# Output projection of the self attention: one fp32 product, or three products of high and low parts in the rounded fp32 type

## The chip, the cores and the metric

The kernel runs on one core of one Trainium2 chip. The time is device time of one execution, in microseconds (us); the median of several runs is compared. Engines: TensorE (PE, with its weight loads as PEld), VectorE (DVE), ScalarE (ACT), GpSimd (POOL) and SyncE (SP), which issues most DMAs. Each engine works through its own queue in order, and the queues meet in semaphores.

## The reference, cut to what matters

x is [8, 512, 256] in fp32. A cross attention to a small context is added to x first. Then a layer of two paths is added, a dense one and a sparse one (a mixture of 8 experts, two of them for each token). The change lies in the dense path:

```python
q, k, v = x @ wq, x @ wk, x @ wv                    # 16 heads of 16
attn = softmax(mask(q k^T / 4))
o = (attn @ v).reshape(b, s, d)                     # [tokens, 256]
h = x + rmsnorm(o @ wo, attn_norm_w)                # o @ wo: the product that changes
ffn = silu(h @ w1) * (h @ w3) @ w2
return h + rmsnorm(ffn, ff_norm_w)
```

## The kernel before

All loops over batches are written out. `in_batches` makes one walk for each step of a software pipeline: a walk (b, c) does the first half of batch b (cross attention, q, k and v, routing, row maxima of the scores) interleaved with the second half of batch c = b - 1 (scores, softmax, output projection, dense network). The first walk has no c, and one more at the end has no b. Behind them come the experts' tiles (`tiles`), and an ending. One list, `STEPS`, gives the order in which every engine's queue takes the steps of a walk; each engine picks those steps in which it has work.

The steps around the change, in the order of the list:

- `cv`, the last product of the cross attention, and on DVE `norm_3`, which normalises the last of four token tiles (`normed`, L1408) once POOL has its reciprocal root (L663);
- `f_o_turn` (of c): PE transposes the attention's output `o_tok` into banks 6 and 7 (`turn`, L844, transposes with `ident`), and ACT copies it into `oT` (`spread`, L1146). `oT` is a part of `room`, a large tile that many stages share;
- `x2_turn` 0 and 1 (of b): the same for the normalised x, in two halves. The second half needs `norm_3`;
- `f_wo` 0 and 1 (L1031): the output projection. For each of four token tiles, 128x256 of output from two products over the halves of the inner dimension; stationary is `oT`, moving is `wo`, both fp32. It waits for both halves of `oT` (`oT_sb`, 2);
- `f_wo_sq`: squares and their sum on ACT (L1244), reciprocal root on POOL; `f_o_norm`: DVE multiplies (L1577) and POOL adds to the residual `hb` (L736); `f_h_turn`: `hb` is transposed and kept as a high part (ACT) and a low part (DVE, L1570) in the rounded fp32 type, called float32r in the code;
- `qk` 0 to 3 (L935): q and k of batch b. ACT, DVE and POOL split each into three bf16 parts, SP writes these to memory and DMAs bring them back spread over partitions (`rep_q`, `rep_k`);
- `v`, `route`, and `fu`/`fg`/`fd`, the dense network: its first product (L1051) is made of three terms, high by high, high by low and low by high, in float32r with 512 columns each;
- `max` (L969, L970): the scores' row maxima, from the parts that came back.

The order on PE is that of the list: what waits at `f_wo` 0 holds up `x2_turn` 1, `f_wo` 1, `qk` and all that follows. In the setup, SP loads the weights (L485: `wo`, `w2`), and in the first walk, ahead of `qk`, DVE reorders `wq` and `wk` (L1473) and scales three norm weights (L1476). POOL makes identity matrices and masks; `mask_kq` (L618, L623) is made and used by nothing.

Of the kernel before, what the change touches and what calls it, by code (L numbers as in the profile page):

```python
# [10 lines left out]
ALU = mybir.AluOpType  # L11
# [6 lines left out]
P = 128  # L18
# [41 lines left out]
    b_ps=G * UNITS, b_exp=G * UNITS, b_cut=G * UNITS, va_ps=G * CHUNKS, av_sb=4, avT_ps=4, o_rec=4, o_nrm=4,  # L60
    oT_ps=2, oT_sb=2, wo_ps=2, wo_sq=2, wo_ri=1, wo_n=2, hb=1, h=2, yb=1, hT_ps=2, hT_sb=2, hT_lo=2,
    fu_ps=16, fu_th=8, fu_u=8, fu_g=8, fd_ps=8, fd_sq=1, fd_ri=1, fd_n=1, y=1, y_out=16, pool_f=2,
# [144 lines left out]
def xattn_ffn(nc, A, out):  # L207
    per = PER
    counted = {}
    with ExitStack() as ctx:  # L210
        def sb(name, shape, dt=F32):
            return ctx.enter_context(nc.sbuf_tensor(name, shape, dt))

        def sem(name):
            return ctx.enter_context(nc.semaphore(name))
# [4 lines left out]
        kv_out = [sem(f"p0_kv_out{i}") for i in range(4)]  # L220
        p0 = {n: sem("p0_" + n) for n in ("w_first", "bias_ps", "w_early", "w_mid", "w_late", "w_turned", "w_up", "kv0_ps", "norms", "split_hi", "split", "ident", "const", "iota", "tr_ps", "tr_sb", "kv_ps", "kv_sb", "bk")}

# [10 lines left out]
        wv = sb("wv", [P, KD, D + E])  # L233
        wo = sb("wo", [P, KD, D])
        w1 = sb("w1", [P, 2, KD, FF], F32R)
# [11 lines left out]
        mask_qk = sb("mask_qk", [P, P], BF16)  # L247
        mask_kq = sb("mask_kq", [P, P], BF16)
        before_b = sb("before_b", [P, P], BF16)
# [17 lines left out]
        with nc.sbuf_tensor("hT", [P, 2, KD, S], F32R) as hT:  # L267
            pass
        room = sb("room", [P, 28672])

        def part(a, n):
            return room[:, a:a + n]
# [19 lines left out]
        scaled = part(3072, 1024).rearrange("p (t d) -> p t d", t=T)  # L292
        oT = part(4096, 1024).rearrange("p (k n) -> p k n", k=KD)
        xh = part(4096, 1024).rearrange("p (t d) -> p t d", t=T)
# [90 lines left out]
        def bank(i, n=512, at=0):  # L385
            return ps[:, i * 512 + at:i * 512 + at + n]
# [11 lines left out]
        def done(ins, name, n=1):  # L398

            counted[name] = counted.get(name, 0) + n  # L400
            return ins.then_inc(sems[name], n)

        def need(eng, b, name, k):

            eng.wait_ge(sems[name], b * per[name] + k + AHEAD.get(name, 0))
# [42 lines left out]
        def _(sp):  # L448
# [30 lines left out]
            def load_late_weights():  # L479
                for dst, src in ((w_heads[:, 0, :, :], "L0_ffn_wq"), (w_heads[:, 1, :, :], "L0_ffn_wk")):  # L480
                    sp.dma_start(dst, A[src].rearrange("(k p) n -> p k n", p=P)).then_inc(p0["w_late"], 16)
                sp.dma_start(wv[:, :, 0:D], A["L0_ffn_wv"].rearrange("(k p) n -> p k n", p=P)).then_inc(p0["w_late"], 16)
                sp.dma_start(wv[:, :, D:D + E], A["L0_ffn_router_w"].rearrange("(k p) n -> p k n", p=P)).then_inc(p0["w_late"], 16)
                for dst, src in ((wo, "L0_ffn_wo"), (w2, "L0_ffn_w2")):
                    sp.dma_start(dst[:, :, :], A[src].rearrange("(k p) n -> p k n", p=P)).then_inc(p0["w_late"], 16)  # L485
                for dst, src in ((aw_bc, "L0_ffn_attn_norm_w"), (fw_bc, "L0_ffn_ff_norm_w"), (mw_bc, "L0_ffn_moe_norm_w")):
                    sp.dma_start(dst[:, :], A[src].partition_broadcast(P)).then_inc(p0["w_late"], 16)
# [120 lines left out]
        def _(pool):  # L608
# [3 lines left out]
            for i, m in enumerate((ident, ident_b)):  # L612
# [3 lines left out]
                                pattern=[[-1, P]], channel_multiplier=1).then_inc(p0["ident"], 1)  # L616
            for m, x in ((mask_qk, 0.0), (mask_kq, 0.0), (before_b, 1.0)):
                g.memset(m[:, :], x).then_inc(p0["ident"], 1)  # L618
            pool.wait_ge(p0["ident"], 7)

            g.affine_select(out=mask_qk[:, :], in_=mask_qk[:, :], compare_op=ALU.is_ge, fill=MASKED, base=0,
                            pattern=[[-1, P]], channel_multiplier=1).then_inc(p0["ident"], 1)
            g.affine_select(out=mask_kq[:, :], in_=mask_kq[:, :], compare_op=ALU.is_ge, fill=MASKED, base=0,  # L623
                            pattern=[[1, P]], channel_multiplier=-1).then_inc(p0["ident"], 1)
            g.affine_select(out=before_b[:, :], in_=before_b[:, :], compare_op=ALU.is_gt, fill=0.0, base=0,
# [178 lines left out]
        def _(pe):  # L804
# [23 lines left out]
            pe.wait_ge(p0["w_mid"], 16 * 2)  # L828
            pe.wait_ge(p0["ident"], 10)
            pe.wait_ge(p0["const"], 9)  # L830
# [5 lines left out]
            def batch(b, c, end=False, only=None):  # L836
# [10 lines left out]
                for step in only or walked(b, c, end):  # L847
# [179 lines left out]
                    elif kind == "f_wo":  # L1027
                        need(pe, c, "oT_sb", 2)
                        for t in (2 * step[1], 2 * step[1] + 1):
                            for k in range(KD):  # L1030
                                last = mm(bank((6, 7)[t // 2], D, t % 2 * D), oT[:, k, t * P:(t + 1) * P], wo[:, k, :], start=(k == 0), stop=(k == KD - 1))  # L1031
                            if t % 2:
                                done(last, "wo_ps")
# [97 lines left out]
        def _(act):  # L1131
# [9 lines left out]
            def batch(b, c, end=False, only=None):  # L1141
                def spread(n, dst, banks, src_name, name, halves=(0, 1)):

                    for t2 in halves:
                        need(act, n, src_name, t2 + 1)
                        done(fn(dst[:, :, t2 * 2 * P:(t2 + 1) * 2 * P], bank(banks[t2]).rearrange("p (k n) -> p k n", k=KD), ACT.Copy), name)  # L1146

                for step in only or walked(b, c, end):
# [87 lines left out]
                    elif kind == "f_o_turn":  # L1236
                        if b is not None:
                            need(act, b, "sc_add", T)
                        spread(c, oT, (6, 7), "oT_ps", "oT_sb")
                    elif kind == "f_wo_sq":  # L1240
# [74 lines left out]
        def _(dve):  # L1315
# [72 lines left out]
            def batch(b, c, end=False, only=None):  # L1388
# [21 lines left out]
                for step in only or walked(b, c, end):  # L1410
# [56 lines left out]
                    elif kind == "qk":  # L1467
                        a = step[1]
                        if a == 0 and c is None:

                            dve.wait_ge(p0["w_late"], 16 * 9)
                            for i, w in enumerate((wq, wk)):
                                v.tensor_copy(w[:, :, :].rearrange("p k (a d h) -> p (k a) d h", a=KD, d=HD),  # L1473
                                              w_heads[:, i, :, :].rearrange("p k (a h d) -> p (k a) d h", a=KD, d=HD)).then_inc(p0["w_turned"], 1)
                            for w in (aw_bc, fw_bc, mw_bc):
                                v.tensor_scalar(w[:, :], w[:, :], float(D) ** 0.5, None, ALU.mult).then_inc(p0["norms"], 1)  # L1476
                            dve.wait_ge(p0["norms"], 3)
                        need(dve, b, "part1", a + 1)
# [79 lines left out]
                    elif kind == "out_t":  # L1558
# [5 lines left out]
                        done(v.tensor_tensor(o_tok[:, :, grp * 64:(grp + 1) * 64].rearrange("p t (j d) -> p t j d", j=4), t4[:, :, :, 0:HD],  # L1564
                                             orec[:, :, :].unsqueeze(3).to_broadcast([P, T, 4, HD]), ALU.mult), "o_nrm")
                    elif kind == "f_h_turn":
                        for t2 in range(2):
# [113 lines left out]
```

## Time and profile before

| | |
|---|---|
| median of 3 runs | 1482.12 us (1478.77 to 1482.25) |
| span of the profiled execution | 1484.5 us |
| PE busy | 1362.4 us, 92% |
| PE weight loads | 882.2 us, 59% |
| DVE, ACT, POOL busy | 810.0, 575.1, 600.2 us |
| mean granted TensorE clock | 0.976 |

The profiled execution is one of its own; its span is 1484.5 us, and the runs' times are of other executions of the same program. Busy time on PE is the union of the MATMUL records with modelled ends, so records that follow one another overlap: for the rate of a group, take the distances of starts. An fp32 product is recorded as two MATMULs with a weight load each, a float32r product or a transpose as one. The granted clock is 1.00 at 2.4 GHz and 0.50 at 1.2 GHz.

### The profile page before, as it was taken

Reading aid. Unit: us, or ns where it says so; the run is one execution under the profiler, and the core shown is the slowest. Engines: PE = TensorE matmul, PEld = TensorE weight load, DVE = VectorE, ACT = ScalarE, POOL = GpSimd, SP = SyncE. Lnnn points to the kernel's source line nnn. Section 1 sums busy time; section 2 is a strip of 40 time slices with the busy share of each in tenths; the row PEclk is TensorE's granted clock in tenths of the full one; section 3 lists DMA queues with packets and bytes.
Section 4 is the critical chain, followed back from the end, with each engine's and each line's share of the span. In section 5 each row is a group of like instructions: output and inputs, shape, how many; then the busy total and the mean of one; then the engine's idle time right before and its main releaser. Section 6 shows DMA issues by size and latency. Waiting matters only on the chain. (4 is left out here: it accounts for less than half of the span.)

```text
span 1484.5 us, 22385 instructions
## 1 busy us (share of the span) xinstructions
PE 1362.4 (92%) x7229; PEld 882.2 (59%) x7230; DVE 810.0 (55%) x1654; ACT 575.1 (39%) x1214; POOL 600.2 (40%) x1051
## 2 busy tenths in 40 slices
PE   6887899899999989998999899999999889999995
PEld 5543556666665666566656665666566346666674
DVE  2625554764585368536753675467537623333348
ACT  2231553055306521642265126503640443344446
POOL 4312353254325342634254225423542445555544
PEclk9998899999999999999999999999999899999997
DMA  6053204110501050106000500140022533322245
GB/s 213 1 153 132 86 1 121 52 30 1 142 30 30 1 156 16 30 8 160 20 15 30 141 17 15 51 121 17 1 83 74 162 107 128 129 87 85 85 186 193
DMA packets 78297, 115.39 MB, mean 78 GB/s; under 512 B 24840, under 2 KB 66208, under 8 KB 75648
## 3 DMA queue, kind: packets, MB, share of 16 engines
q1 hardware_dynamic: 67888, 79.69, 17.9%
q10 hardware_dynamic: 3840, 16.78, 4.2%
q0 software_dynamic: 6480, 17.77, 3.3%
q8 instruction: 52, 0.85, 0.2%
q14 instruction: 37, 0.30, 0.1%
HBM read 70.22 MB, written 43.59 MB: 77 GB/s over the span
## 5 line engine op out<-in xcount | busy, mean ns | idle before, releaser
L1540 DVE TENSOR_REDUCE nm<-ps 128x2 f32<-128x256 f32 (+3 forms) x256 | 202.5, 819 | 85.6 <-PE ps L970 79.5
L1229 ACT ACTIVATE room<-ps 128x512 f32<-128x512 f32 x320 | 179.8, 599 | 151.3 <-PE ps L996 151.1
L1051 PE MATMUL ps<-hT,w 128*128 128x512 f32 x768 | 206.5, 412 | 0.0
L703 POOL TENSOR_SCALAR_AFFINE_SELECT room<-room 128x256 f32<-128x256 f32 (+1 forms) x320 | 121.0, 390 | 136.4 <-ACT room L1229 131.7
L969 PE MATMUL ps<-room 96*128 96x128 bf16 (+3 forms) x512 | 127.9, 312 | 35.7 <-DMA room<-parts_d 17.8
L1051 PEld LDWEIGHTS ps<-hT,w 128*128 128x128 f32 x768 | 140.4, 190 | 32.1 <-DVE hT L1570 2.0
L1061 PE MATMUL ps<-w,room 128*128 128x256 f32 x512 | 137.8, 400 | 7.8 <-DVE room L1591 7.8
L1253 ACT ACTIVATE room<-ps 128x512 f32<-128x512 f32 x64 | 37.2, 593 | 277.2 <-PE ps L1051 277.2
L1087 PE MATMUL ps<-room 128*128 x284 | 135.4, 599 | 1.8 <-ACT room L1281 1.8
L920 PE MATMUL ps<-room 128*128 128x256 f32 x512 | 123.1, 384 | 2.8 <-ACT room L1190 1.8
L901 PE MATMUL ps<-room,xnT 128*128 128x512 f32 x256 | 122.0, 601 | 0.0
L996 PE MATMUL ps<-room 99*128 99x384 bf16 (+3 forms) x512 | 111.0, 306 | 8.7 <-ACT room L1229 6.4
L969 PEld LDWEIGHTS ps<-room 96*128 96x128 bf16 x512 | 50.9, 100 | 97.9 <-DVE nm L1540 41.1
L920 PEld LDWEIGHTS ps<-room 128*128 128x128 f32 x512 | 93.8, 190 | 22.7 <-issue 6.7
L1061 PEld LDWEIGHTS ps<-w,room 128*128 128x128 f32 x512 | 91.9, 195 | 24.1 <-DVE room L1591 11.5
L970 PE MATMUL ps<-mask_qk,ident_b 128*128 128x128 bf16 x512 | 104.6, 225 | 0.0
L1634 DVE COPY room<-ps 128x256 f32<-128x256 f32 x71 | 30.1, 424 | 125.9 <-PE ps L1095 117.7
L1441 DVE TENSOR_TENSOR room<-ps,room 128x1024 f32<-128x1024 f32 x32 | 39.1, 1222 | 106.0 <-PE ps L901 106.0
L996 PEld LDWEIGHTS ps<-room 99*128 99x128 bf16 x512 | 42.9, 98 | 88.0 <-issue 44.7
L1009 PE MATMUL ps<-room,v_aug 128*32 128x512 f32 (+3 forms) x1024 | 90.6, 449 | 3.0 <-POOL room L703 2.0
L652 POOL TENSOR_TENSOR spare_p<-neg_half 128x1 f32<-128x1 f32 x95 | 18.3, 192 | 179.7 <-DVE room L1533 114.6
L794 POOL DMA_INDIRECT pair_d<-room,ids_u x71 | 71.8, 1011 | 33.7 <-issue 30.5
(236 smaller groups left out, 2360.1 us busy)
## 6 DMA issues: line engine op xcount, KB each, us to landing
room<-parts_d SPq DMA_DIRECT2D x48, 256.0 KB, 8.7
room<-parts_d ACTq DMA_DIRECT2D x48, 256.0 KB, 6.2
room<-xs_d SPq DMA_DIRECT2D x71, 129.0 KB
parts_d<-room SPq DMA_DIRECT2D x64, 128.0 KB, 1.8
room<-pair_d SPq DMA_DIRECT2D x8, 1024.0 KB, 7.8
room<-in_L_ffn_ew SPq DMA_DIRECT2D x24, 256.0 KB, 5.5
xin<-in_x SPq DMA_DIRECT2D x8, 512.0 KB, 11.3
parts_d<-xnT SPq DMA_DIRECT2D x32, 128.0 KB, 1.8
```

Source lines behind the costliest of these rows:

```text
L703: done(g.affine_select(out=w, in_=w, compare_op=ALU.is_ge, fill=0.0, base=0, pattern=[[0, 2]] * (blocks - 1) + [[1, P]], channel_multiplie ...
L901: last = mm(bank(half), xnT[:, k, t * P:(t + 1) * P], m_sb[:, k, half * 512:(half + 1) * 512], start=(k == 0), stop=(k == KD - 1))
L920: last = mm(bank(3, D), pT[:, t % 2, a * P:(a + 1) * P], vw[:, a, :], start=(a == 0), stop=(a == PAIRS - 1))
L969: mm(bank(o, n), q_rep[0:KREP, rep_at(h), t * P:n], k_rep[0:KREP, rep_at(h), 0:n], start=True, stop=False)
L970: last = mm(bank(o, P, t * P), ident_b[:, :], mask_qk[:, :], start=False, stop=True)
L996: last = mm(ps[:, o:o + S - kb * P], k_rep[0:KREP + MROWS, h, kb * P:(kb + 1) * P], q_rep[0:KREP + MROWS, h, kb * P:S], start=True, stop=T ...
L1009: last = mm(ps[32 * j:32 * j + 32, 4 * 512 + kb * P:5 * 512], v_aug[:, v_at(kb, 4 * grp + j):v_at(kb, 4 * grp + j) + 32], prob[:, at:at + ...
L1051: last = mm(bank(up_banks(b, m)[i]), w[:, x, k, m * P:(m + 1) * P], hT[:, y, k, :], start=((x, y, k) == terms[0]), stop=((x, y, k) == term ...
L1061: last = mm(bank((6, 7)[half], D, t % 2 * D), gT[:, m % 2, t * P:(t + 1) * P], w2[:, m, :], start=(m == 0 and t % 2 == 0), stop=(m == FB - ...
L1087: last = mm(bank(2 + i % 2), xsT[:, i % 2, k * P:(k + 1) * P], ew[:, bass.ds(at + k * 2 * D, 2 * D)], start=(k == 0), stop=(k == KD - 1))
L1229: done(fn(prob[:, u * 512:(u + 1) * 512], bank(score_bank(b) + n % 2), ACT.Exp), "b_exp")
L1540: done(v.tensor_reduce(nm[:, t, 2 * hp:2 * hp + 2], pair_ps, AX.X, ALU.max, negate=True), "a_max")
```

## The change

`wo` is kept as a high part (the value rounded to float32r) and a low part (the rest). The fp32 matrix is loaded into a part of `room` (`wo_in`), and DVE makes the two parts in the first walk. `oT` becomes a high part, written by ACT in the same place as before, and a low part, which DVE makes in a new step of its own in `f_o_turn`: two subtractions of 128x512 from the banks. `f_wo` makes three terms for each half of the inner dimension: 6 products of 256 columns for a token tile where there were two fp32 ones, and waits for the low part (`oT_lo`, 2). The two new tiles lie in `room`'s space, which is laid over them. `mask_kq` goes, and one semaphore is used for two purposes.

```diff
--- before.py
+++ after.py
@@ -58,7 +58,7 @@
     gmax=1, gexp=1, mask=1, rank_ps=1, slot=1, xk=1, scat=128, dve_step=42, pool_a=4, pool_n=1,
     a_ps=32, a_max=32, m_part=2, mT_ps=2, mT_sb=2, m_row0=48, m_row1=48,
     b_ps=G * UNITS, b_exp=G * UNITS, b_cut=G * UNITS, va_ps=G * CHUNKS, av_sb=4, avT_ps=4, o_rec=4, o_nrm=4,
-    oT_ps=2, oT_sb=2, wo_ps=2, wo_sq=2, wo_ri=1, wo_n=2, hb=1, h=2, yb=1, hT_ps=2, hT_sb=2, hT_lo=2,
+    oT_ps=2, oT_sb=2, oT_lo=2, wo_ps=2, wo_sq=2, wo_ri=1, wo_n=2, hb=1, h=2, yb=1, hT_ps=2, hT_sb=2, hT_lo=2,
     fu_ps=16, fu_th=8, fu_u=8, fu_g=8, fd_ps=8, fd_sq=1, fd_ri=1, fd_n=1, y=1, y_out=16, pool_f=2,
 )
 
@@ -218,7 +218,7 @@
 
         sems = {n: sem(n) for n in per}
         kv_out = [sem(f"p0_kv_out{i}") for i in range(4)]
-        p0 = {n: sem("p0_" + n) for n in ("w_first", "bias_ps", "w_early", "w_mid", "w_late", "w_turned", "w_up", "kv0_ps", "norms", "split_hi", "split", "ident", "const", "iota", "tr_ps", "tr_sb", "kv_ps", "kv_sb", "bk")}
+        p0 = {n: sem("p0_" + n) for n in ("w_first", "bias_ps", "w_early", "w_mid", "w_late", "w_turned", "w_up", "kv0_ps", "split_hi", "split", "ident", "const", "iota", "tr_ps", "tr_sb", "kv_ps", "kv_sb", "bk")}
 
         moe = {n: sem("moe_" + n) for n in ("table_step", "table", "ids_off", "ids", "ew_in", "zero", "gate", "xT_ps", "xT", "up_ps", "th", "u", "g", "gT_ps", "gT", "dn_ps", "eo")}
         xs_in = [sem(f"xs_in{i}") for i in range(4)]
@@ -231,7 +231,7 @@
         wq = sb("wq", [P, KD, D])
         wk = sb("wk", [P, KD, D])
         wv = sb("wv", [P, KD, D + E])
-        wo = sb("wo", [P, KD, D])
+        wo = sb("wo", [P, 2, KD, D], F32R)
         w1 = sb("w1", [P, 2, KD, FF], F32R)
         w3 = sb("w3", [P, 2, KD, FF], F32R)
         w2 = sb("w2", [P, FB, D])
@@ -245,7 +245,6 @@
         ident = sb("ident", [P, P])
         ident_b = sb("ident_b", [P, P], BF16)
         mask_qk = sb("mask_qk", [P, P], BF16)
-        mask_kq = sb("mask_kq", [P, P], BF16)
         before_b = sb("before_b", [P, P], BF16)
         ones_b = sb("ones_b", [P, P], BF16)
         neg_half = sb("neg_half", [P, T])
@@ -266,6 +265,8 @@
 
         with nc.sbuf_tensor("hT", [P, 2, KD, S], F32R) as hT:
             pass
+        with nc.sbuf_tensor("oT_lo", [P, KD, S], F32R) as oT_lo, nc.sbuf_tensor("below_oT", [P, 3072], F32), nc.sbuf_tensor("oT_hi", [P, KD, S], F32R) as oT_hi:
+            oT = (oT_hi, oT_lo)
         room = sb("room", [P, 28672])
 
         def part(a, n):
@@ -290,7 +291,7 @@
         gT = part(3072, 1024).rearrange("p (i n) -> p i n", i=2)
         squares = part(2048, 1024).rearrange("p (t d) -> p t d", t=T)
         scaled = part(3072, 1024).rearrange("p (t d) -> p t d", t=T)
-        oT = part(4096, 1024).rearrange("p (k n) -> p k n", k=KD)
+        wo_in = part(22528, KD * D).rearrange("p (k n) -> p k n", k=KD)
         xh = part(4096, 1024).rearrange("p (t d) -> p t d", t=T)
 
         wq_c = part(11264, 2048).rearrange("p (k n) -> p k n", k=KD)
@@ -481,8 +482,8 @@
                     sp.dma_start(dst, A[src].rearrange("(k p) n -> p k n", p=P)).then_inc(p0["w_late"], 16)
                 sp.dma_start(wv[:, :, 0:D], A["L0_ffn_wv"].rearrange("(k p) n -> p k n", p=P)).then_inc(p0["w_late"], 16)
                 sp.dma_start(wv[:, :, D:D + E], A["L0_ffn_router_w"].rearrange("(k p) n -> p k n", p=P)).then_inc(p0["w_late"], 16)
-                for dst, src in ((wo, "L0_ffn_wo"), (w2, "L0_ffn_w2")):
-                    sp.dma_start(dst[:, :, :], A[src].rearrange("(k p) n -> p k n", p=P)).then_inc(p0["w_late"], 16)
+                for dst, src in ((wo_in, "L0_ffn_wo"), (w2[:, :, :], "L0_ffn_w2")):
+                    sp.dma_start(dst, A[src].rearrange("(k p) n -> p k n", p=P)).then_inc(p0["w_late"], 16)
                 for dst, src in ((aw_bc, "L0_ffn_attn_norm_w"), (fw_bc, "L0_ffn_ff_norm_w"), (mw_bc, "L0_ffn_moe_norm_w")):
                     sp.dma_start(dst[:, :], A[src].partition_broadcast(P)).then_inc(p0["w_late"], 16)
 
@@ -614,14 +615,12 @@
                 pool.wait_ge(p0["ident"], 2 * i + 1)
                 g.affine_select(out=m[:, :], in_=m[:, :], compare_op=ALU.not_equal, fill=1.0, base=0,
                                 pattern=[[-1, P]], channel_multiplier=1).then_inc(p0["ident"], 1)
-            for m, x in ((mask_qk, 0.0), (mask_kq, 0.0), (before_b, 1.0)):
+            for m, x in ((mask_qk, 0.0), (before_b, 1.0)):
                 g.memset(m[:, :], x).then_inc(p0["ident"], 1)
-            pool.wait_ge(p0["ident"], 7)
+            pool.wait_ge(p0["ident"], 6)
 
             g.affine_select(out=mask_qk[:, :], in_=mask_qk[:, :], compare_op=ALU.is_ge, fill=MASKED, base=0,
                             pattern=[[-1, P]], channel_multiplier=1).then_inc(p0["ident"], 1)
-            g.affine_select(out=mask_kq[:, :], in_=mask_kq[:, :], compare_op=ALU.is_ge, fill=MASKED, base=0,
-                            pattern=[[1, P]], channel_multiplier=-1).then_inc(p0["ident"], 1)
             g.affine_select(out=before_b[:, :], in_=before_b[:, :], compare_op=ALU.is_gt, fill=0.0, base=0,
                             pattern=[[1, P]], channel_multiplier=-1).then_inc(p0["ident"], 1)
             g.memset(neg_half[:, :], -0.5).then_inc(p0["const"], 1)
@@ -826,7 +825,7 @@
                         last = mm(bank(6 + i % 2, CK, a * CK), w[:, k, pa * P:(pa + 1) * P], ctxT[:, k, 0:CK], start=(k == 0), stop=(k == KD - 1))
                 last.then_inc(p0["kv0_ps"], 1)
             pe.wait_ge(p0["w_mid"], 16 * 2)
-            pe.wait_ge(p0["ident"], 10)
+            pe.wait_ge(p0["ident"], 8)
             pe.wait_ge(p0["const"], 9)
             pe.wait_ge(p0["iota"], 4)
 
@@ -1025,10 +1024,14 @@
                             before(pe, c, "fd_n")
                         turn(c, o_tok, (6, 7), lambda t2: [("o_nrm", G)], "oT_ps")
                     elif kind == "f_wo":
-                        need(pe, c, "oT_sb", 2)
+                        need(pe, c, "oT_lo", 2)
+                        if c == 0:
+                            pe.wait_ge(p0["w_turned"], 4)
+                        terms = [(x, y, k) for x, y in ((0, 0), (0, 1), (1, 0)) for k in range(KD)]
                         for t in (2 * step[1], 2 * step[1] + 1):
-                            for k in range(KD):
-                                last = mm(bank((6, 7)[t // 2], D, t % 2 * D), oT[:, k, t * P:(t + 1) * P], wo[:, k, :], start=(k == 0), stop=(k == KD - 1))
+                            for x, y, k in terms:
+                                last = mm(bank((6, 7)[t // 2], D, t % 2 * D), oT[x][:, k, t * P:(t + 1) * P], wo[:, y, k, :],
+                                          start=((x, y, k) == terms[0]), stop=((x, y, k) == terms[-1]))
                             if t % 2:
                                 done(last, "wo_ps")
                     elif kind == "f_h_turn":
@@ -1236,7 +1239,7 @@
                     elif kind == "f_o_turn":
                         if b is not None:
                             need(act, b, "sc_add", T)
-                        spread(c, oT, (6, 7), "oT_ps", "oT_sb")
+                        spread(c, oT[0], (6, 7), "oT_ps", "oT_sb")
                     elif kind == "f_wo_sq":
                         for i in range(2):
                             need(act, c, "wo_ps", i + 1)
@@ -1472,9 +1475,12 @@
                             for i, w in enumerate((wq, wk)):
                                 v.tensor_copy(w[:, :, :].rearrange("p k (a d h) -> p (k a) d h", a=KD, d=HD),
                                               w_heads[:, i, :, :].rearrange("p k (a h d) -> p (k a) d h", a=KD, d=HD)).then_inc(p0["w_turned"], 1)
+                            v.tensor_copy(wo[:, 0, :, :], wo_in).then_inc(p0["w_turned"], 1)
+                            dve.wait_ge(p0["w_turned"], 3)
+                            v.tensor_tensor(wo[:, 1, :, :], wo_in, wo[:, 0, :, :].bitcast(F32), ALU.subtract).then_inc(p0["w_turned"], 1)
                             for w in (aw_bc, fw_bc, mw_bc):
-                                v.tensor_scalar(w[:, :], w[:, :], float(D) ** 0.5, None, ALU.mult).then_inc(p0["norms"], 1)
-                            dve.wait_ge(p0["norms"], 3)
+                                v.tensor_scalar(w[:, :], w[:, :], float(D) ** 0.5, None, ALU.mult).then_inc(p0["w_turned"], 1)
+                            dve.wait_ge(p0["w_turned"], 7)
                         need(dve, b, "part1", a + 1)
                         if a >= 2:
                             need(dve, b, "part3", a - 1)
@@ -1563,6 +1569,12 @@
                         need(dve, c, "o_rec", grp + 1)
                         done(v.tensor_tensor(o_tok[:, :, grp * 64:(grp + 1) * 64].rearrange("p t (j d) -> p t j d", j=4), t4[:, :, :, 0:HD],
                                              orec[:, :, :].unsqueeze(3).to_broadcast([P, T, 4, HD]), ALU.mult), "o_nrm")
+                    elif kind == "f_o_turn":
+                        for t2 in range(2):
+                            need(dve, c, "oT_sb", t2 + 1)
+                            cols = slice(t2 * 2 * P, (t2 + 1) * 2 * P)
+                            done(v.tensor_tensor(oT[1][:, :, cols], bank(6 + t2).rearrange("p (k n) -> p k n", k=KD),
+                                                 oT[0][:, :, cols].bitcast(F32), ALU.subtract), "oT_lo")
                     elif kind == "f_h_turn":
                         for t2 in range(2):
                             need(dve, c, "hT_sb", t2 + 1)
```

## Rows read from the trace of the kernel before

**Rows 1.** Page, part 1: busy us, share of the span, instructions.

```profile
PE 1362.4 (92%) x7229; PEld 882.2 (59%) x7230; DVE 810.0 (55%) x1654; ACT 575.1 (39%) x1214; POOL 600.2 (40%) x1051
```

**Rows 2.** Windows, one walk: stretch, length, busy by engine, clock, DMA share.

```profile
597.00:740.00 143.00, 134.83 (x780) 89.35 (x780) 84.29 (x170) 55.27 (x111) 56.19 (x82) 1.00 0.19 53
```

**Rows 3.** Waits of PE: us in total, times, longest.

```profile
PE ps L969 <- DMA room<-parts_d: 17.8, 7, 3.8
```

**Rows 4.** Timeline around f_wo of one walk: start us, us, instructions, idle before.

```profile
227.35 1.04 PE L844 MATMUL ps<-ident,o_tok 128*128 128x128 f32 x8
228.04 1.08 ACT L1146 ACTIVATE room<-ps 128x512 f32<-128x512 f32 x2 [3.96 <-PE ps L844]
228.22 0.60 PE L844 MATMUL ps<-ident,xn_id 128*128 128x128 f32 x4
...
229.18 1.99 PE L1031 MATMUL ps<-wo,room 128*128 128x256 f32 x8 [0.36 <-ACT room L1146]
229.66 0.41 DVE L1408 TENSOR_SCALAR xn_id<-x,mv,rs 128x256 f32<-128x256 f32 x1 [0.71 <-POOL rs L663]
...
231.45 1.89 PE L1031 MATMUL ps<-wo,room 128*128 128x256 f32 x8
...
233.18 3.60 PE L935 MATMUL ps<-xn2T,wq 128*128 128x512 f32 x8
```

**Rows 5.** Source view of L1031: duration ns min/median/max, first and last start.

```profile
L1031 PE MATMUL ps<-wo,room x128: 379/379/484, 229.2 to 1205.0; 128*128 128x256 f32 x128
```

**Rows 6.** L1051 (float32r): timeline of PE, then its source view.

```profile
245.70 5.64 PE L1051 MATMUL ps<-hT,w 128*128 128x512 f32 x23
...
L1051 PE MATMUL ps<-hT,w x768: 388/397/776, 245.7 to 1461.0; 128*128 128x512 f32 x192
```

**Rows 7.** Timeline of L826, fp32 records of 64 columns.

```profile
14.82 7.36 PE L826 MATMUL ps<-room 128*128 128x64 f32 x64 [0.69 <-ACT room L1140]
```

**Rows 8.** Source view of L1570, the low part of hT.

```profile
L1570 DVE TENSOR_TENSOR hT<-ps,hT x16: 678/686/691, 244.4 to 1213.7; 128x512 fp32r<-128x512 f32 x16
```

**Rows 9.** Timeline, the low part of hT and the product behind it.

```profile
244.35 1.29 DVE L1570 TENSOR_TENSOR hT<-ps,hT 128x512 fp32r<-128x512 f32 x2 [2.16 <-ACT hT L1146]
...
245.70 0.50 PE L1051 MATMUL ps<-hT,w 128*128 128x512 f32 x1
```

**Rows 10.** Timeline, the projection's norm and the residual add.

```profile
234.64 1.02 POOL L663 TENSOR_TENSOR ri<-ve_f,neg_half 128x4 f32<-128x4 f32 x1
...
238.05 1.65 DVE L1577 SCALAR_TENSOR_TENSOR o_tok<-ps,ri,aw_bc 128x256 f32<-128x256 f32 x4
...
240.84 2.50 POOL L736 TENSOR_TENSOR hb<-hb,o_tok 128x512 f32<-128x512 f32 x2
```

**Rows 11.** Windows at three waits before max and behind them.

```profile
260.17:263.17 3.00, 0.00 (x1) 0.02 (x1) 0.51 (x3) 0.60 (x1) 0.19 (x1) 1.00 0.91 227
263.17:267.00 3.83, 3.82 (x16) 2.75 (x17) 1.42 (x3) 0.00 (x0) 1.08 (x1) 0.59 0.13 43
...
834.97:841.00 6.03, 6.03 (x22) 4.27 (x23) 2.30 (x4) 0.00 (x0) 2.04 (x2) 0.53 0.07 24
...
977.20:979.60 2.40, 0.06 (x2) 0.08 (x2) 0.50 (x3) 0.60 (x1) 0.19 (x1) 1.00 0.86 212
979.60:984.20 4.60, 4.60 (x19) 3.23 (x20) 2.30 (x4) 0.00 (x0) 1.70 (x2) 0.63 0.09 31
```

**Rows 12.** Windows at such a wait in another walk.

```profile
543.00:549.00 6.00, 2.77 (x17) 2.05 (x15) 2.62 (x15) 0.60 (x1) 0.19 (x1) 1.00 0.76 178
```

**Rows 13.** Timeline of the first walk: DVE at qk.

```profile
84.16 0.69 DVE L1481 SCALAR_TENSOR_TENSOR xin<-ps,xnT 128x512 f32<-128x512 f32 x1 [3.98 <-ACT xnT L1196]
```

**Rows 14.** Source view of L623, a mask.

```profile
L623 POOL TENSOR_SCALAR_AFFINE_SELECT mask_kq<-mask_kq x1: 292/292/292, 3.2 to 3.2; 128x128 bf16<-128x128 bf16 x1
```

**Rows 15.** Timeline of the last walk, around f_wo.

```profile
1200.52 1.09 ACT L1146 ACTIVATE room<-ps 128x512 f32<-128x512 f32 x2 [2.27 <-PE ps L844]
...
1206.27 0.41 PE L1078 MATMUL ps<-ident,room 128*128 128x128 f32 x2 [0.89 <-DMA room<-xs_d]
```

## The prediction

> **What bounds the kernel now.** I read four views, in this order. The page first: PE is busy 92% of the span, DVE 55%, and no other engine comes near [rows 1]. Then the table by walk: a walk of one batch takes some 143 us and PE is busy in about 135 of them; seven walks have this stretch and are alike, so one read closely stands for all [rows 2]. Then the releasers of PE's idle time: the largest is the first score product of the "max" stage (L969), 17.8 us in 7 times, on a DMA that brings q and k back [rows 3]. Last the timeline around the projection (L1031) in one walk [rows 4], where the argument is; the reader is to see that PE runs there with one idle stretch of 0.36 us, and which two rows of ACT and DVE stand beside it. The kernel is bound by PE in program order: what makes PE wait, or work longer, lengthens the walk unless a later wait swallows it.
>
> **What goes and comes on PE.** One fp32 product of 256 columns is two MATMUL records, so f_wo has 8 + 8 records in a walk. Eight of them take 1.89 us, of which 0.38 is the last one's own duration: (1.89 - 0.38) / 7 = 0.216 us apart, 16 x 0.216 = 3.46 us in a walk [rows 4, 5]. In the new form each token tile has 3 terms x 2 halves of the inner dimension = 6 records, 24 in a walk. The trace has no rounded product of 256 columns. The nearest rows: the rounded product of 512 columns, 23 records in 5.64 us, (5.64 - 0.40) / 22 = 0.238 apart [rows 6]; and the fp32 records of 64 columns with a weight load of 128 each, 64 in 7.36 us, (7.36 - 0.28) / 63 = 0.112 apart (twice 64 columns stream in 0.053, so that is the pace of the loads) [rows 7]. So a rounded record streams a column per cycle at 2.4 GHz (512 columns are 213 ns) with some 18 to 25 ns over it, where the fp32 one makes two passes of its 256. For 256 columns the stream is 107 ns, and I take 0.125 us apart (half of 0.213, and 0.018 over it, the nearest of the terms). The bounds are 0.112 (the pace of the loads) and 0.238 (the width doesn't matter). 24 x 0.125 = 3.00 us: PE saves 0.46 us in a walk, between 0.77 saved and 2.25 lost by the bounds.
>
> The Trainium skill ("TensorE: Matmul & The Clock Gate", Measured speedup vs the span model) says that a weight load overlaps matmuls in flight only when it targets other row groups; here all use all rows. By its load time (LDWEIGHTS section: 128 columns at 1.2 GHz, an estimate of 107 ns), load and stream would add to 0.214 us a record. The 0.238 us at 512 columns speaks against it: added, that would be 0.320.
>
> **The new wait.** Before, f_wo 0 began when ACT had copied both halves of the transposed output: copies 228.04 to 229.12, product at 229.18 [rows 4]. Now the low part has to be there too: two subtractions of 128x512 on DVE, the same operation as the low part of hT, mean 686 ns [rows 8]; the pair runs 1.29 us, and PE begins 0.06 us behind it (244.35 + 1.29 = 245.64, L1051 at 245.70) [rows 9]. They stand in DVE's queue behind norm_3, the last normalised token tile, which waits for POOL's reciprocal root and runs 229.66 to 230.07 [rows 4]. ACT's copies are done long before. So the subtractions run from 230.03 (DVE overlaps neighbours by some 0.05) to 231.32, and f_wo 0 begins at 231.38, not 229.18: **2.2 us later**. Queued behind it on PE: x2_turn 1, f_wo 1, qk. x2_turn 1 needs norm_3 (230.07) and could have run at once; it stands behind the waiting product and hides nothing. Until 231.38 PE has nothing else in its order.
>
> From f_wo 0 to qk it is 233.18 - 229.18 = 4.00 us now: 3.46 of products, and 0.54 of four transposes and the joints. It becomes 3.00 + 0.54 = 3.54. So qk begins at 231.38 + 3.54 = 234.92 instead of 233.18: **+1.74 us in a walk**.
>
> **Does a later wait give it back?** The only large one is the DMA before "max" (17.8 / 7 = 2.5 us in the mean, 3.8 at most) [rows 3]. It would, if that DMA were anchored ahead of f_wo. It isn't: what it brings are the parts of q and k, made from the products of qk by ACT, DVE and POOL and then written to memory, and the last two stand in POOL's queue behind the residual add (240.84), which needs the normed output of this same projection [rows 10]. qk, the parts, the DMA and max all move by the same 1.74 us. The norm of the projection (POOL's root, ready at 234.64 + 1.02 = 235.66) is used by DVE at 238.05, 2.4 us of slack; both ends move alike. Nothing late before is early now. Seven walks have this stretch (b = 1 to 7): 7 x 1.74 = **12.2 us**.
>
> **The clock.** The new gap of PE runs from the end of x2_turn 0 (228.82) to 231.38, 2.56 us, where it was 0.36. PE's granted clock is 1.00 in the walks but for a few drops to half (1.2 GHz), and those follow such gaps. Before "max": 3.00 us idle, then a mean of 0.59 over the next 3.83 us; some 2.3 us idle, then 0.63 over 4.6; and 0.53 over the 6.03 us behind the longest wait [rows 11]. A wait of some 3.2 us in another walk was followed by none [rows 12], and so were the remaining ones of the seven. Three drops from seven waits, all from waits above 2 us. Mine lies among the short ones, but transposes, not products, fill the 1.47 us before it. A drop costs half of what it covers, (1 - 0.63) x 4.6 = 1.7 us, and it would fall on dense products. I take 2 of 7: **3.4 us**; none to five is 0 to 8.5.
>
> **The edits outside.** The split of wo in the first walk is a copy and a subtraction of 128x512 on DVE (0.6 to 0.7 us each, by rows 8), some 1.3 us together, behind the copies that PE waits for and ahead of rest1, for which DVE idles 3.98 us until ACT's copy at 84.1 [rows 13]: nothing; uncovered it would be 1.3 once. The load of wo goes to another address with the same bytes; the mask's two POOL instructions go, the longer 0.29 us at 3.2 us of the span [rows 14], and PE doesn't wait for POOL in the setup: between 0 and 0.5 gained, I take 0. In the last walk, with no cross attention beside it, DVE is free: ACT's second copy ends at 1201.61 and the second subtraction at about 1202.45, so f_wo starts some 0.85 us later and saves 0.46; the 0.4 us left fall into the 0.89 us for which PE then waits for a DMA [rows 15]. Nothing.
>
> **Sum.** 12.2 + 3.4 = 15.6 us on the profiled span of 1484.5, which gives 1500.1. That execution is 2.4 us above the median of the runs, 1482.12; on the median it is 1497.7. I forecast **1498 us**.
>
> **Rivals.** (1) The rounded product at 256 columns costs as much as load and stream together, or its width doesn't matter: 0.216 to 0.238 a record. For: nothing in the trace shows this width. Against: the wider rounded products [rows 6] overlap their loads, and loads alone come every 0.112 [rows 7]. Then f_wo takes 5.2 to 5.7 us instead of 3.46, a walk grows by 2.2 + 1.7 to 2.2 = 3.9 to 4.4, seven by 27 to 31: 1509 to 1513, with the drops up to 1516. (The skill's rule on loads, were it true, is at the low end of this.) Chance 0.08.
> (2) The other side: the wait before "max" swallows the stall. If what ends last there is not the chain from qk but a DMA that stands on something earlier (the memory's pace, the SP queue), then PE reaches it 1.74 us later and waits up to 1.74 less. It decides from where the DMA's landing doesn't move with qk. For: the DMA share is 0.91 and 0.86 in two of these waits [rows 11], so the DMA engines are nearly full. Against: they are filled by this batch's own parts. The shorter gaps then also spare the three drops there, 5 us: 1477 to 1483. Chance 0.08, of which 0.04 faster and 0.04 the same.
> (3) My forecast's mechanism, with everything between no drop and five and 0.112 to 0.15 us a record: 7 x (2.2 - 0.77) = 10.0 without a drop, 1492.1; 7 x (2.2 + 0.15) = 16.5 with five drops, 1507. Chance 0.82. A remaining 0.02 is spread over surprises of both signs.
>
> **Range and chances.** 1489 to 1508 holds case 3 and a little; the two rivals outside are 0.16. About 0.3% (4.4 us) can be told from no change: faster 0.05, same 0.05, slower 0.90.
>
> **What would show it.** In the profile after: f_wo with 24 records in a walk, about 0.125 us apart, a PE gap of about 2.5 us before it put down to DVE's subtraction, DVE's pair of subtractions directly behind norm_3, qk 1.7 us later behind x2_turn 0, the wait before "max" unchanged at some 2.5 us, walks longer by 1.7 to 3.5 us, and half-clock stretches right behind f_wo's gap in one to four walks. The forecast is wrong if PE's gap before f_wo is under 1 us, if the records are 0.2 us apart, or if the wait before "max" shrinks by as much as qk moves.

## The result, and the profile after

| | before | after |
|---|---|---|
| median | 1482.18 us (4 runs) | 1502.23 us (4 runs, 1499.6 to 1509.8) |
| ratio of the times | | 1.0137 (95% interval 1.0102 to 1.0171) |
| span of the profiled execution | 1484.5 us | 1502.8 us |
| PE busy | 1362.4 us | 1372.2 us |
| mean granted clock | 0.976 | 0.966 |

The change makes the kernel 20 us slower. The forecast was 1498 us, slower with a chance of 0.90. One run of e3 below (1547 us) and one of the kernel before beside it (6109 us) were slow ones, and are left out of the medians and ratios.

Part 1 of the page after [rows 1 before]: PE is busy 10 us longer, with 64 records more, and DVE has 18 more, 16 of them the new subtractions and two the split of `wo`.

```profile
PE 1372.2 (91%) x7293; PEld 895.2 (60%) x7294; DVE 821.1 (55%) x1672; ACT 574.9 (38%) x1214; POOL 599.8 (40%) x1049
```

The waits of PE after (in total, times, longest) [rows 3 before]. A wait that was not there is now the largest: all eight f_wo wait for the low part, 19.1 us. The wait before max on the parts from memory is 13.8 us in 6 times, where it was 17.8 in 7.

```profile
PE ps L1033 <- DVE oT_lo L1576: 19.1, 8, 2.5
...
PE ps L968 <- DMA room<-parts_d: 13.8, 6, 2.9
```

The timeline around f_wo in one walk after (start us, us, count, idle before) [rows 4 before]. The reader is to see the order on DVE: norm_3 (L1411) behind its wait for POOL, then the two subtractions at once, then PE 0.05 us behind their end; and on PE nothing between the transposes of 520.78 and 523.88. ACT's copies had ended at 521.69.

```profile
519.91 1.04 PE L843 MATMUL ps<-ident,o_tok 128*128 128x128 f32 x8
...
520.61 1.08 ACT L1149 ACTIVATE oT_hi<-ps 128x512 fp32r<-128x512 f32 x2 [3.96 <-PE ps L843]
...
520.78 0.60 PE L843 MATMUL ps<-ident,xn_id 128*128 128x128 f32 x4
...
522.22 0.41 DVE L1411 TENSOR_SCALAR xn_id<-x,mv,rs 128x256 f32<-128x256 f32 x1 [0.71 <-POOL rs L662]
522.55 1.28 DVE L1576 TENSOR_TENSOR oT_lo<-ps,oT_hi 128x512 fp32r<-128x512 f32 x2
...
523.88 0.74 PE L1033 MATMUL ps<-wo,oT_hi 128*128 128x256 f32 x4 [2.50 <-DVE oT_lo L1576]
524.46 0.40 PE L1033 MATMUL ps<-wo,oT_lo 128*128 128x256 f32 x2
...
527.03 0.40 PE L1033 MATMUL ps<-wo,oT_lo 128*128 128x256 f32 x2
527.27 3.17 PE L934 MATMUL ps<-xn2T,wq 128*128 128x512 f32 x7
```

From f_wo 0 to the first product of qk it is 527.27 - 523.88 = 3.39 us here, where it was 4.00. But this is the one walk of seven where the clock held. Windows over the gap and over f_wo to qk, in the walk before and in this one (stretch, length, busy by engine, granted clock, DMA share): the same 28 records (24 products and 4 transposes) take 4.93 us at a mean clock of 0.65, or 3.39 at 1.00. The gap itself is 2.50 us in both.

```profile
372.92:375.42 2.50, 0.00 (x1) 0.00 (x0) 1.74 (x4) 0.80 (x2) 0.73 (x2) 1.00 0.02 7
375.43:380.36 4.93, 4.93 (x28) 4.93 (x29) 0.00 (x0) 1.22 (x5) 0.00 (x0) 0.65 0.00 0
521.38:523.88 2.50, 0.00 (x1) 0.00 (x0) 1.74 (x4) 0.80 (x2) 0.73 (x2) 1.00 0.00 0
523.88:527.27 3.39, 3.38 (x29) 3.39 (x29) 0.00 (x0) 1.22 (x5) 0.00 (x0) 1.00 0.00 0
```

The starts of the steps on PE, read from both traces for all seven walks with this stretch, split the walk in five. In us, before and after:

| stretch on PE | before, each walk | after, each walk | seven walks, after minus before |
|---|---|---|---|
| f_o_turn to f_wo 0 | 1.83 | 3.98 | +15.0 |
| f_wo 0 to qk | 4.00 | 3.38 once, 4.81 to 4.94 six times | +4.8 |
| qk to the dense network (first L1054) | 12.52 | 12.52 | 0.0 |
| dense network to max | 16.1 to 18.3 | 16.0 to 17.7 | -2.3 |
| max to the next f_o_turn | 77.4 to 109.4 | 77.3 to 109.6 | +1.0 |
| before the first and behind the last | | | -0.2 |

They sum to 18.3 us, the difference of the spans. The second line is two things: 7 x 0.62 = 4.3 us saved by the products, and 9.1 lost in six walks at half clock. The last three are small and of both signs; the stretches that differ between walks contain the wait for memory and an occasional drop of the clock. The -0.2 is -2.4 ahead of the first walk and +2.2 behind the last; the first f_o_turn starts anywhere from 222.6 to 227.3 us in the ten profiles of this case.

### The profile page after: what moved, and what is told of

Read it like the earlier page. It is cut to its first block and busy times, and to the rows that moved or that the text cites. A ratio compares the mean times of both kernels' runs of the same rounds, so it can differ in the third digit from the quotient of the medians.

```text
span 1502.8 us, 22530 instructions
## 1 busy us (share of the span) xinstructions
PE 1372.2 (91%) x7293; PEld 895.2 (60%) x7294; DVE 821.1 (55%) x1672; ACT 574.9 (38%) x1214; POOL 599.8 (40%) x1049
## 3 DMA queue, kind: packets, MB, share of 16 engines
q1 hardware_dynamic: 67888, 79.69, 17.7%
## 5 line engine op out<-in xcount | busy, mean ns | idle before, releaser
L1054 PE MATMUL ps<-hT,w 128*128 128x512 f32 x768 | 208.5, 415 | 0.0
L1054 PEld LDWEIGHTS ps<-hT,w 128*128 128x128 f32 x768 | 142.0, 192 | 32.6 <-DVE hT L1582 2.0
L651 POOL TENSOR_TENSOR spare_p<-neg_half 128x1 f32<-128x1 f32 x95 | 18.3, 192 | 182.2 <-DVE room L1539 117.1
```

What stands on the lines that cost most here:

```text
L1054: last = mm(bank(up_banks(b, m)[i]), w[:, x, k, m * P:(m + 1) * P], hT[:, y, k, :], start=((x, y, k) == terms[0]), stop=((x, y, k) == term ...
```

## The experiments

Theory A: the loss is PE's wait for DVE's low part, which ends 2.15 us behind the old start in each walk because the subtractions stand behind norm_3, and the half clock that follows the gap; the rounded products themselves save 0.62 us a walk. Theory B: the products are the costly part. Ratios are to runs of the kernel before on the same chip. The gap is PE's idle time just before f_wo 0; a drop is a stretch at half clock (1.2 GHz) that begins around the start of f_wo, behind that gap. Gaps, drops and the stretch f_wo to qk are read from each kernel's own trace, which is one execution; how many drops the other executions had is not known.

| kernel | median us | ratio (95%) | gap before f_wo | drops of 7 |
|---|---|---|---|---|
| changed, again | 1504.01 | 1.0129 (1.0080 to 1.0178) | 2.50 | 7 |
| e1 wait, fp32 products | 1503.95 | 1.0143 (1.0112 to 1.0175) | 2.50 | 3 |
| e2 no low part | 1478.07 | 0.9960 (0.9939 to 0.9981) | 0.36 | 0 |
| e3 gap filled | 1494.38 | 1.0085 (1.0052 to 1.0119) | filled, 0.61 left | 0 |
| e7 high terms first | 1479.70 | 0.9966 (0.9943 to 0.9988) | 0.36 | 0 |
| e4 low part ahead of norm_3 | 1486.30 | 1.0030 (1.0005 to 1.0054) | 1.38 | 0 |
| e5 half by half | 1499.32 | 1.0115 (1.0078 to 1.0152) | 1.90 | 6 |
| e6 both | 1479.95 | 0.9984 (0.9957 to 1.0010) | 0.78 | 0 |

The median of the kernel before was 1483.6 beside the first four (e1, e2, e3, e7) and 1483.1 beside the others.

**e1, the wait alone.** To the kernel before, the DVE step is added and f_wo waits for it:

```diff
-                        need(pe, c, "oT_sb", 2)
+                        need(pe, c, "oT_lo", 2)
...
+                    elif kind == "f_o_turn":
+                        for t2 in range(2):
+                            need(dve, c, "oT_sb", t2 + 1)
+                            cols = slice(t2 * 2 * P, (t2 + 1) * 2 * P)
+                            done(v.tensor_tensor(oT_lo[:, :, cols], bank(6 + t2)..., oT[:, :, cols], ALU.subtract), "oT_lo")
```

> The kernel before with only the low part and its wait: DVE makes the two subtractions of 128x512 in f_o_turn, f_wo waits for them and then makes the old fp32 products (the low part is used by nothing). Theory A (the wait for DVE, and the half clock behind it, make the loss; the rounded products save 0.62 us in a walk): the gap before f_wo is 2.5 us as in the changed kernel, f_wo to qk is 4.00 us where the clock holds and about 5.5 where it drops, so 7 x 2.15 = 15 us and 1.5 us for each drop; with six drops 1482 + 15 + 9 = 1506 us, between 1500 and 1510, some 4 us above the changed kernel. Theory B (the three rounded products are the costly part, the wait is mostly hidden): within 5 us of 1482.

1503.95 us. All of the loss is there without one rounded product. PE's wait is that of the changed kernel (L1571 is the new subtraction, whose tile lies in `room` here):

```profile
PE ps L1032 <- DVE room L1571: 19.1, 8, 2.5
```

Windows over f_wo to qk, in a walk at full clock and in one that drops to half:

```profile
517.54:521.54 4.00, 4.00 (x21) 3.54 (x22) 0.00 (x0) 1.33 (x5) 0.00 (x0) 1.00 0.00 0
662.24:667.91 5.67, 5.67 (x20) 4.77 (x21) 0.00 (x0) 1.32 (x5) 0.00 (x0) 0.70 0.00 0
```

Theory B is out. The 4 us that theory A expected above the changed kernel don't show in the times: the profiled execution had three drops where the changed kernel's had six and seven, and three or four drops less, at 1.5 us, are worth about as much as the 4.3 us that the rounded products save. But that execution was the second fastest of six (1501.41 us, granted clock 0.975); three others took 1505 to 1508 us at 0.969 or 0.970, so three drops need not be the usual number. Whether the same gap drops the clock less often ahead of fp32 products stays open.

**e2, the products alone.** DVE's step is left out, and the high part stands in for the low one:

```diff
-                        need(pe, c, "oT_lo", 2)
+                        need(pe, c, "oT_sb", 2)
...
-                                last = mm(..., oT[x][:, k, t * P:(t + 1) * P], wo[:, y, k, :],
+                                last = mm(..., oT[0][:, k, t * P:(t + 1) * P], wo[:, y, k, :],
```

> The changed kernel without the low part of oT: DVE's two subtractions are left out, f_wo waits for ACT's copies only, and the two products of low by high take the high part in the low part's place, so one term of the projection is wrong and all 24 records stay. Theory A: no gap, no drop behind it, f_wo to qk 3.4 us against 4.00: 1482 - 7 x 0.62 = 1478 us (1475 to 1480). Theory B: 24 records cost more than 16, above 1490 us.

1478.07 us, 5.5 below its kernel before (5.9 by the ratio); 7 x 0.62 = 4.3 were expected, inside the interval. No walk has a drop at f_wo, and f_wo to qk is 3.38 us in all seven:

```profile
511.94:515.32 3.38, 3.38 (x28) 3.38 (x29) 0.41 (x1) 1.66 (x6) 0.45 (x1) 1.00 0.00 0
653.84:657.22 3.38, 3.38 (x29) 3.38 (x29) 0.41 (x1) 1.66 (x6) 0.45 (x1) 1.00 0.00 0
```

**e3, the clock alone.** The wait stays; PE gets work in the gap:

```diff
+                        if step[1] == 0 and b is not None:
+                            for _ in range(34):
+                                mm(bank(4, P), ident_b[:, :], mask_qk[:, :], start=True, stop=True)
                         need(pe, c, "oT_lo", 2)
```

> The changed kernel, with 34 bf16 products of 128 columns (mask by identity, into a bank that nothing reads) put ahead of f_wo 0 in the seven walks, where PE waits anyway: some 1.9 us of work in a gap of 2.5. Nothing that f_wo waits for moves. Theory A with the clock as a cost of its own: no half clock at f_wo, f_wo to qk 3.4 us in all walks instead of 4.8 to 4.9 in six of seven: 6 x 1.45 = 8.7 us less, about 1493 us (1490 to 1496). Rival C (the drops cost nothing, since what follows waits for others): the time of the changed kernel, 1500 to 1504.

1494.38 us, inside the expected stretch. By the ratios it is 7.7 and 6.5 us below the two measurements of the changed kernel; 8.7 were expected. The interval of its ratio (to 1.0119) meets that of the first measurement (from 1.0102) and overlaps that of the second (from 1.0080), so the size is rough; the trace is not. The timeline of PE shows the filling, and f_wo at the same distance from the transposes as in the changed kernel:

```profile
514.34 2.06 PE L1029 MATMUL ps<-mask_qk,ident_b 128*128 128x128 bf16 x34
517.01 0.74 PE L1036 MATMUL ps<-wo,oT_hi 128*128 128x256 f32 x4 [0.61 <-DVE oT_lo L1579]
...
520.39 1.02 PE L934 MATMUL ps<-xn2T,wq 128*128 128x512 f32 x2
```

f_o_turn to f_wo 0 is 3.98 us as in the changed kernel, f_wo to qk 3.38 in all seven. What is left above the kernel before, 12.6 us by the ratio, is the wait less the saving: 15.0 - 4.3 = 10.7. So the clock is a loss of its own, and work that is used by nothing took it away.

**e4, DVE's order.** In walks with a second half, norm_3 moves behind the subtractions:

```diff
                     elif kind == "norm_3":
-                        normed(T - 1)
+                        if c is None:
+                            normed(T - 1)
...
                     elif kind == "f_o_turn":
...
+                        if b is not None:
+                            normed(T - 1)
```

> The changed kernel with DVE's order turned: in walks with a second half, norm_3 stands behind the two subtractions instead of ahead of them. Theory A (the stall is DVE's two subtractions plus the wait of norm_3 for POOL ahead of them): the subtractions run from 228.95 to 230.2 in the old walk's times, f_wo begins 1.1 us later than before instead of 2.15, the gap is 1.4 us, too short to drop the clock; a walk is 1.1 - 0.62 = 0.45 us longer than before, seven 3.2: 1483 + 3 = 1486 us (1484 to 1491). Theory A' (the subtractions alone are the stall, norm_3's place is nothing): as the changed kernel, 1500 to 1504.

1486.30 us, as expected. The timeline shows the subtractions in DVE's place of waiting for POOL, norm_3 behind them, and PE 1.1 us sooner:

```profile
516.16 1.28 DVE L1577 TENSOR_TENSOR oT_lo<-ps,oT_hi 128x512 fp32r<-128x512 f32 x2
...
517.35 0.40 DVE L1411 TENSOR_SCALAR xn_id<-x,mv,rs 128x256 f32<-128x256 f32 x1
...
517.49 0.74 PE L1033 MATMUL ps<-wo,oT_hi 128*128 128x256 f32 x4 [1.38 <-DVE oT_lo L1577]
```

Of the 16 to 18 us gained over the changed kernel 7.8 are the shorter wait (f_o_turn to f_wo 2.86 instead of 3.98, seven times); the rest, 8 to 10 us, is near what six or seven drops cost at 1.5 us, and none of the seven walks drops here.

**e5, half by half.** One word of the wait:

```diff
-                        need(pe, c, "oT_lo", 2)
+                        need(pe, c, "oT_lo", step[1] + 1)
```

> The changed kernel, with f_wo 0 waiting for the first half of the low part only and f_wo 1 for the second. Theory A: f_wo begins 0.63 us sooner than in the changed kernel, with a gap of 1.9 us; 1.5 - 0.62 = 0.9 us a walk above before, 6.4 in seven, 1489, and 1.5 for each drop of the clock that a gap of 1.9 us still brings (none to four): 1489 to 1495. Rival C (the gap's length does not matter to the clock): six drops, 1498.

1499.32 us. Theory A's range was missed: the wait is shorter by 0.6 us as expected, but a gap of 1.90 us still brought the half clock in six of seven walks. Rival C's number came out (six drops, 1498), its reason did not: in e4 and e6, where the gap is shorter still, none of the seven walks drops. The timeline of PE at such a gap,

```profile
518.48 0.75 PE L1033 MATMUL ps<-wo,oT_hi 128*128 128x256 f32 x4 [1.90 <-DVE oT_lo L1576]
```

and the windows over f_wo to qk in this walk and the next:

```profile
518.48:523.38 4.90, 4.90 (x28) 4.90 (x29) 0.54 (x1) 1.33 (x5) 0.00 (x0) 0.66 0.00 0
665.36:670.29 4.93, 4.93 (x28) 4.93 (x29) 0.54 (x1) 1.33 (x5) 0.00 (x0) 0.65 0.00 0
```

**e6, both of these.**

> Both: the subtractions ahead of norm_3, and each half of f_wo waits for its half. Theory A: the first subtraction ends at about 229.6, f_wo begins 0.45 us later than before and saves 0.62 behind it: 0.15 us a walk less, no drop: 1482 us (1479 to 1485), no difference from before that can be told. Rival D (x2_turn 1 or qk waits for the later norm_3): 0.5 us a walk more, 1486.

1479.95 us, as expected, and the same as before within the interval. The gap is 0.78 us, f_o_turn to f_wo 2.25, f_wo to qk 3.38 in the seven walks:

```profile
511.45 0.74 PE L1033 MATMUL ps<-wo,oT_hi 128*128 128x256 f32 x4 [0.78 <-DVE oT_lo L1577]
```

**e7, high terms first.** f_wo 0 makes the two terms of the high part for all four token tiles, f_wo 1 the term of the low part, into banks 4 and 5, so that DVE can still read banks 6 and 7:

```diff
-                        need(pe, c, "oT_lo", 2)
+                        low = step[1]
+                        need(pe, c, ("oT_sb", "oT_lo")[low], 2)
...
-                        terms = [(x, y, k) for x, y in ((0, 0), (0, 1), (1, 0)) for k in range(KD)]
-                        for t in (2 * step[1], 2 * step[1] + 1):
+                        terms = [(x, y, k) for x, y in (((0, 0), (0, 1)), ((1, 0),))[low] for k in range(KD)]
+                        for t in range(T):
                             for x, y, k in terms:
-                                last = mm(bank((6, 7)[t // 2], D, t % 2 * D), oT[x]...
+                                last = mm(bank((4, 5)[t // 2], D, t % 2 * D), oT[x]...
...
```

> The changed kernel with f_wo in another order and other banks: f_wo 0 makes the high-by-high and high-by-low terms of all four token tiles, into banks 4 and 5, and waits for ACT's copies only; then x2_turn 1; f_wo 1 makes the low-by-high terms, waiting for DVE. Theory A: 16 records (1.9 us) and four transposes (0.44) fill PE from 229.2 to 231.5, when the low part is just there; qk comes 0.6 us earlier than in the kernel before, no gap, no drop: 1482 - 4.3 = 1478 us (1475 to 1481). Rival D (the shared banks 4 and 5, or the wait of x2_turn 1 for norm_3, put a new wait in its place): 1482 or more.

1479.70 us, ratio 0.9966 (0.9943 to 0.9988): faster than the kernel before and than the changed one. The timeline: PE starts behind ACT's copies again, and by the time 16 records and four transposes are done the subtractions have ended (514.89), so the low terms wait for nothing that matters.

```profile
512.80 2.16 PE L1034 MATMUL ps<-wo,oT_hi 128*128 128x256 f32 x16 [0.36 <-ACT oT_hi L1150]
...
513.61 1.28 DVE L1577 TENSOR_TENSOR oT_lo<-ps,oT_hi 128x512 fp32r<-128x512 f32 x2
...
514.79 0.60 PE L843 MATMUL ps<-ident,xn_id 128*128 128x128 f32 x4
...
515.15 1.20 PE L1034 MATMUL ps<-wo,oT_lo 128*128 128x256 f32 x8
```

**The changed kernel again.**

> The changed kernel once more, for a second profile. Theory A: the gap of 2.50 us in all seven walks and f_wo to qk 3.38 where the clock holds, 4.8 to 4.9 where it drops; how many of the seven drop is left open, between three and seven. The span goes with that number, 1.5 us each.

1504.01 us; the profiled execution has the gap of 2.50 us and a drop in all seven walks, and a span of 1509.2, where the first had six and 1502.8. It was the slowest of its four runs; the fastest took 1497.03 us at a granted clock of 0.976, against 0.964 here, a sign that the number of drops varies from one execution to the next. Two of its windows, f_wo to qk:

```profile
377.84:382.76 4.92, 4.92 (x28) 4.92 (x29) 0.00 (x0) 1.33 (x5) 0.00 (x0) 0.65 0.00 0
524.61:529.54 4.93, 4.93 (x29) 4.93 (x29) 0.00 (x0) 1.33 (x5) 0.00 (x0) 0.65 0.00 0
```

One drop more accounts for 1.5 of the 6.4 us between the two spans; the rest lies in other stretches (half clock for 112 us in all instead of 105) and in what differs from one execution to the next.

## Why the prediction was right, step by step

- **The new wait**: put at 2.2 us a walk, behind norm_3 and the two subtractions. It is 3.98 - 1.83 = 2.15. e1 has it without the rounded products, e4 takes half of it away by DVE's order alone. Right in place and size.
- **The products**: put at 0.125 us a record and 0.46 saved. In the walk at full clock the records stand 0.118 us apart (the median of the 24), f_wo to qk is 3.38, and 0.62 is saved. The bound of 0.112 was nearly reached. The 0.018 us that the prediction laid over the stream of 0.107 stands in none of its rows, of which rows 6 give 0.025 for 512 columns; measured is 0.011. The rule on loads that was weighed there is from the Trainium skill, "TensorE: Matmul & The Clock Gate", section The mechanism (the prediction names the section behind it): a load overlaps products in flight only when its row group is another. With the load time that this page of the Trainium skill gives under LDWEIGHTS, the rule would make 0.214 us a record, an estimate. The traces speak against it at this width: the median distance at full clock is 0.117 or 0.118 us in the changed kernel, e2, e3 and e7 alike.
- **No later wait gives it back**: right. qk to the dense network is 12.52 us in every walk of both kernels, and the wait before max, 2.5 us in the mean, is 2.3 in six walks and 0.8 in the seventh. The 2.3 us by which the stretch to max shrank in all is not the 12 that the rival needed, and in e1, with the same delay of f_wo, the wait before max is 17.8 us as before.
- **The clock**: the step that was mis-sized. Put at 2 drops of 7 at 1.7 us each, 3.4 us, with one to four as the sign to look for; it was 6 and 7 of 7 in the two profiled executions, 9.1 us in the first, at 1.43 to 1.56 each. The count was taken from the waits before max, where three of seven had a drop. That group did not stand for this gap: there PE works on dense products up to the wait, here 1.47 us of transposes come first. Whether these are the reason was not tried. That a shorter gap keeps the clock up in these walks is shown: none of seven drops at 1.38 us (e4) and 0.78 (e6), six at 1.90 (e5). That the length alone decides is not: 2.50 us brought seven, six and three drops, and in the last walk (below) a drop followed a gap of 1.57 us in four of five profiles.
- **The edits outside, and the last walk**: nothing expected, and nothing clear of noise seen in the times. PE's wait at the first qk is 0.78 us, as before. In the last walk, f_wo begins 0.83 us later behind f_o_turn, as forecast (0.85), but the clock was overlooked there: behind a gap of 1.57 us its 24 products ran at a mean clock of 0.62, and PE's next work began 7.10 us after f_o_turn instead of 6.41. So 0.7 us, not nothing; the forecast had the delay absorbed by the wait for a DMA, and the drop used that up. The timelines there, changed kernel and e4, which has the same gap and kept the clock (the first four products take 1.22 and 0.74 us):

```profile
1218.57 1.22 PE L1033 MATMUL ps<-wo,oT_hi 128*128 128x256 f32 x4 [1.57 <-DVE oT_lo L1576]
...
1201.54 0.74 PE L1033 MATMUL ps<-wo,oT_hi 128*128 128x256 f32 x4 [1.57 <-DVE oT_lo L1577]
```

With the measured terms the sum is 1482.2 + 7 x 2.15 - 7 x 0.62 + 9.1 = 1502.0, against 1502.23. The agreement is better than it can claim, since it lays the terms of one execution on a median; the spans themselves differ by 18.3 us. The forecast of 1498 came within 4.2 us, and in part by luck: too little saved (1.1 us in seven walks) and too few drops (5.7 us) are errors of opposite sign.

## What to carry to other kernels

Splitting an operand into high and low parts adds a step on another engine in front of the product, and here, where PE bounds the kernel in program order, that step cost its whole uncovered length, with what stood ahead of it in that engine's queue. The cheaper product paid, clear of noise, where the terms that need no low part went first and covered the step (e7); with a shorter wait it came out even (e6). When a gap appears in PE's work, ask what the clock does behind it: here a gap of 1.9 us cost 1.5 us more in six of seven walks. Filling a gap with products that nothing reads is a quick test of whether that is happening.

## What the runs showed of the hardware

A rounded fp32 product of 128x128 by 256 columns comes every 0.118 us at full clock, load included, and every 0.213 at half (medians); 256 columns at 2.4 GHz are 0.107 us, so it is nearly the pace of its columns. An fp32 product of this size is two records 0.216 us apart, 3.7 times the cost. Three rounded terms of 256 columns cost 0.35 us where one fp32 product costs 0.43.

In the seven walks alike, the half clock came behind gaps of 2.5 us in 6, 7 and 3 (the changed kernel twice, e1), of 1.9 us in 6, and of 1.4, 0.8, 0.6 and 0.4 us in none (e4, e6, e3, e2 and e7). In the last walk, where PE had also waited 0.72 and 0.90 us shortly before, a gap of 1.57 us was followed by it in four of five profiles (not in e4), and in e5 and e6, with a gap of 0.56 us, it had set in some 2 us before f_wo. So these are observations of this lead-in, not a threshold. One drop cost 1.5 us in f_wo with rounded products and 1.7 with fp32 ones.
